# Five transposes of a pipelined graph network: from the tensor engine to 32x32 block turns on the vector engine and copies by DMA

## The reference

```
x = layernorm(x + L0(x, adj))   # attention, 8 heads of 16, edge bias, then W_o
x = layernorm(x + L1(x, adj))   # convolution of 17 taps, exp(-distance) messages, GRU gates
x = layernorm(x + L2(x, adj))   # additive attention: u = adj*exp(e_i+f_j), normalised by rows
x = layernorm(x + L3(x, adj))   # graph attention, 4 heads of 32, leaky relu, masked softmax
```

## Time and profile before

| | |
|---|---|
| median of three runs | 1429.56 us (1428.88 to 1431.28) |
| profiled execution, its own time | 1432.08 us |
| its span | 1430.3 us |
| mean granted TensorE clock | 0.976 |
| busy: PE, DVE, ACT, POOL | 1352.1, 1191.3, 1188.4, 663.1 us |
| DMA | 46.86 MB, 33 GB/s |

### The profile page before, as it was taken

The page is one execution under the profiler, slowest core; times in us unless marked ns, Lnnn a source line. Parts: engine busy times, 40 slices in busy tenths (PEclk is TensorE's granted clock), DMA queues, the critical chain, the costliest instruction groups (busy, mean ns, idle before and its releaser), DMA issues.

```text
span 1430.3 us, 40514 instructions
## 1 busy us (share of the span) xinstructions
PE 1352.1 (95%) x13178; PEld 1075.1 (75%) x13267; DVE 1191.3 (83%) x3407; ACT 1188.4 (83%) x4353; POOL 663.1 (46%) x1014
## 2 busy tenths in 40 slices
PE   4799999999999999999999999999999999999964
PEld 3577788877778887777888777788877778887642
DVE  6568888888888888888888888888888888886763
ACT  3867888889888888998888899888889988887654
POOL 1133445554444555444455544445554444555532
PEclk7899999999999999999999999999999999999986
DMA  3100110011111001111100111111011111100000
GB/s 117 38 31 31 31 31 17 16 39 38 39 38 39 25 16 39 38 38 39 39 29 12 39 39 38 38 39 34 6 39 39 38 39 38 33 8 16 9 15 23
DMA packets 23825, 46.86 MB, mean 33 GB/s; under 512 B 2753, under 2 KB 2754, under 8 KB 23490
## 3 DMA queue, kind: packets, MB, share of 16 engines
q1 hardware_dynamic: 23618, 44.27, 9.8%
HBM read 35.88 MB, written 8.39 MB: 31 GB/s over the span
## 4 chain that ended last, share of the span: by engine, by line
PE 78%; DVE 10%; POOL 5%; issue 4%; ACT 3%; DVEq 0%; POOLq 0%; ACTq 0%
PE B L591 18%; PE B L689 14%; PE B L499 12%; PE B L537 5%; PE B L558 4%; DVE B L1353 4%; DVE x L1326 3%; POOL rstd L376 3%; PE B L808 2%; PE B L523 2%; PE B L788 2%; PE B L754 2%; PE B L581 2%; PE B L665 2%; PE B L683 2%
## 5 line engine op out<-in xcount | busy, mean ns | idle before, releaser
L995 ACT ACTIVATE e<-B,nm 128x128 f32<-128x128 f32 x1024 | 363.9, 385 | 12.5 <-DVE nm L1361 12.0
L499 PEld LDWEIGHTS B<-ident,e 128*128 128x128 f32 x1536 | 187.0, 144 | 104.3 <-issue 75.7
L499 PE MATMUL B<-ident,e 128*128 128x128 f32 x1536 | 230.0, 281 | 9.2 <-ACT e L1151 3.9
L995 ACT ACTIVATION_READ_ACCUMULATOR e<-B,nm 128x1 f32 x1024 | 231.9, 226 | 0.0
L1353 DVE SCALAR_TENSOR_TENSOR B<-an,rowb,mask 128x512 f32<-128x512 f32 x256 | 194.2, 794 | 19.0 <-ACT pT L1004 9.5
L1151 ACT ACTIVATE e<-l,nm 128x128 f32<-128x128 f32 x512 | 198.9, 400 | 10.0 <-DVE nm L1582 9.9
L1361 DVE TENSOR_REDUCE nm<-B 128x4 f32<-128x512 f32 x256 | 166.5, 683 | 35.0 <-PE B L537 34.8
L1004 ACT ACTIVATE pT<-B 128x512 f32<-128x512 f32 x256 | 157.9, 617 | 44.5 <-PE B L499 41.3
L373 POOL TENSOR_TENSOR veps<-meanv,eps 128x4 f32<-128x4 f32 x128 | 41.8, 326 | 328.9 <-DVE meanv L1320 328.8
L376 POOL TENSOR_TENSOR rstd<-veps,neghalf 128x4 f32<-128x4 f32 x128 | 139.7, 1092 | 10.0
L1582 DVE TENSOR_REDUCE nm<-l 128x4 f32<-128x512 f32 x128 | 87.0, 679 | 41.9 <-ACT l L1141 41.9
(11 more groups left out here) (201 smaller groups left out, 3471.1 us busy)
## 6 DMA issues: line engine op xcount, KB each, us to landing
xt<-in_x_t SPq DMA_DIRECT2D x32, 256.0 KB, 3.1
an<-in_adj_n SPq DMA_DIRECT2D x32, 256.0 KB, 2.7
xn<-in_x_n SPq DMA_DIRECT2D x32, 256.0 KB, 3.3
at<-in_adj_t SPq DMA_DIRECT2D x32, 256.0 KB, 3.2
out_x<-xo SPq DMA_DIRECT2D x32, 256.0 KB, 3.5
wm<-in_mats SPq DMA_DIRECT2D x1, 1088.0 KB, 9.4
wm<-in_mats SPq DMA_DIRECT2D x1, 832.0 KB, 7.1
wm<-in_mats SPq DMA_DIRECT2D x1, 320.0 KB, 3.0
```

What stands on the lines that cost most here:

```text
L499: last = mm(g(dst, b), g(src, b), ident[:, :], is_transpose=True, start=(b == 0), stop=True, skip_group_check=True)
L995: last = fn(g(e0[:, h % 2, :], b), g(bank, b), ACT.Exp, bias=nm0[:, h % 4, b:b + 1], accum_out=sum0[s % 2][:, b, head(h):head(h) + 1])
```

## The change

The turn is split in two. DVE turns each 32x32 block of a tile in itself (`v.transpose`, in the order rows STREAM_TRANSPOSE), which leaves the blocks in their old places. DMA then moves the blocks: the tile is written whole to DRAM (128 rows of 2 KB, `write_blocks`) and read back in four transfers (`read_blocks`), one for each 32 partitions, in which every run of 32 numbers, 128 bytes, goes to its new place: 4 x 32 x 4 x 4 = 2048 runs a tile. For the inverse sums it is one turn of a 128x32 tile, four small writes and one read that repeats each row for 16 partitions. The tiles `x1b`, `yb`, `x3b`, `o3b`, `recb` take the turned blocks, `yn` and `o3n` the moved ones. `turn_out3` reads the PSUM bank directly, so the copy `keep_out3` goes as well.

Gone are five tile transposes a group on PE, four copies a group on ACT and `spread_sums` on POOL. DVE gets five turns a group. SP gets 25 DMAs a group, with waits between write and read. The order of every engine's step is written anew, with other bank assignments.

```diff
+            def write_blocks(s, done, sent, got, here, there):
...
+                wait(sp, q[got], MOVED * s)
+                sp.wait_ge(q[done], s + 1)
+                sp.dma_start(there[:, :], here[:, :]).then_inc(q[sent], DMA)
+
+            def read_blocks(s, sent, got, there, here):
+
+                sp.wait_ge(q[sent], DMA * (s + 1))
+                for c in range(4):
+                    sp.dma_start(here[32 * c:32 * c + 32, :].rearrange("r (b i j) -> r b i j", b=GB, i=4),
+                                 there.rearrange("(i r) (b c j) -> c r b i j", i=4, b=GB, c=4)[c]).then_inc(q[got], DMA)
+
+            def write_sums(s):
...
+                for i in range(4):
+                    sp.dma_start(inv_mem.rearrange("h (b i j) -> i (h b) j", b=GB, i=4)[i],
+                                 recb[32 * i:32 * i + 32, :]).then_inc(q["rb_sent"], DMA)
+
+            def read_sums(s):
...
+                sp.dma_start(recT[:, :], inv_mem.unsqueeze(1).broadcast_to([H0, D0, GB * N])).then_inc(q["recT_got"], DMA)
...
+            def read_x1(s):
...
+                wait(sp, q["v1_done"], s)
+                wait(sp, q["zx_done"], s)
...
+                wait(sp, q["ghn_ps"], s)
+                read_blocks(s, "x1_sent", "x1T_ready", x1_mem, x1T)
...
             def step(t):
+                write_x3(t - 5)
+                read_x3(t - 5)
+                load_at(t - 3)
+                write_y(t - 4)
+                read_y(t - 4)
+                write_out3(t - 6)
+                store(t - 8)
                 load_xt(t)
+                load_xn(t - 1)
                 load_an(t)
-                load_xn(t)
-                store(t - 8)
-                load_at(t - 1)
+                read_out3(t - 6)
+                write_x1(t - 2)
+                read_x1(t - 2)
+                write_sums(t - 1)
+                read_sums(t - 1)
...
-                pe.wait_ge(ln_out[0], s + 1)
-                transpose4(bank, x1).then_inc(q["x1t_ps"], 1)
...
-                pe.wait_ge(q["x1T_ready"], s + 1)
+                pe.wait_ge(q["x1T_ready"], MOVED * (s + 1))
                 mm(bank[:, :], wm[:, W1:W1 + N], x1T[:, :], start=True, stop=True).then_inc(q["c1_ps"], 1)
...
-                fn(x1T[:, :], bank[:, :], ACT.Copy).then_inc(q["x1T_ready"], 1)
...
+            def turn_x1(s):
...
+                wait(dve, q["x1_sent"], DMA * s)
+                dve.wait_ge(ln_out[0], s + 1)
+                v.transpose(x1b[:, :], x1[:, :]).then_inc(q["x1b_done"], 1)
...
+            def turn_out3(s, bank):
...
+                wait(dve, q["o3_sent"], DMA * s)
+                dve.wait_ge(q["pv3_ps"], s + 1)
+                v.transpose(o3b[:, :], bank[:, :]).then_inc(q["o3b_done"], 1)
```

More of the change, by code:

```diff
@@ L43 @@
 DMA = 16
-STEPS = GROUPS + 16
+MOVED = 4 * DMA
+STEPS = GROUPS + 8
 (C_G1, C_B1, C_M1, C_V1, C_G2, C_B2, C_M2, C_V2, C_BIR, C_BIZ, C_BIN, C_BHR, C_BHZ, C_BHN, C_A1, C_A2,
@@ L561, in values @@
                 last.then_inc(q["pv_ps"], 1)
-            def sums_T(s, bank, users):
-                if not live(s):
-                    return
-                freed(pe, s, users)
-                pe.wait_ge(q["recx_done"], s + 1)
-                for b in range(GB):
-                    last = mm(g(bank, b), recx[:, b, :, :].rearrange("p h d -> p (h d)"), ident[:, :], is_transpose=True,
-                              start=(b == 0), stop=True, skip_group_check=True)
-                last.then_inc(q["recT_ps"], 1)
             def project_out(s, bank, users):
@@ L1111, in exp_edges @@
                 fn(eg[:, :, :], h2[:, :, N:HC], ACT.Exp).then_inc(q["eg_ready"], 1)
-            def keep_x3(s, bank):
-                if not live(s):
-                    return
-                wait(act, q["h3_ps"], s)
-                wait(act, q["ej_ps"], s)
-                act.wait_ge(q["x3t_ps"], s + 1)
-                fn(x3T[:, :], bank[:, :], ACT.Copy).then_inc(q["x3T_ready"], 1)
             def keep_h3(s, bank):
@@ L1488, in gru_out, with turn_y, stats1 @@
                 v.tensor_tensor(yT[:, :], zn[:, :], zx[:, :], ALU.add).then_inc(q["y_done"], 1)
-            def stats1(s, bank):
+            def turn_y(s):
+                if not live(s):
+                    return
+                wait(dve, q["y_sent"], DMA * s)
+                dve.wait_ge(q["y_done"], s + 1)
+                v.transpose(yb[:, :], yT[:, :]).then_inc(q["yb_done"], 1)
+            def stats1(s):
                 if not live(s):
@@ L1500, in aggr1, with norm1 @@
                 ln_aggregate(1, s)
[L1502 removed]
+            def norm1(s):
                 if not live(s):
@@ L1572, in norm2, with turn_x3 @@
                     return
-                wait(dve, q["x3t_ps"], s - 1)
+                wait(dve, q["x3b_done"], s - 1)
                 wait(dve, q["r3_done"], s - 1)
                 ln_apply(2, s, r2, x3[s % 2])
+            def turn_x3(s):
+                if not live(s):
+                    return
+                wait(dve, q["x3_sent"], DMA * s)
+                dve.wait_ge(ln_out[2], s + 1)
+                v.transpose(x3b[:, :], x3[s % 2][:, :]).then_inc(q["x3b_done"], 1)
             def row_max3(s, b):
@@ new lines, in step @@
+                stats3(t - 8)
+                row_max(t - 2, 7, B[7])
+                stats1(t - 5)
+                aggr3(t - 8)
+                invert_sums3(t - 7)
+                aggr1(t - 5)
+                row_max3(t - 6, 0)
+                row_max3(t - 6, 1)
+                hidden_bias(t - 5, (B[6], B[0]))
+                edge_mask3(t - 3)
+                norm1(t - 5)
+                norm0(t - 3)
+                turn_x1(t - 3)
+                hidden_times_e(t - 5)
+                norm3(t - 8)
```

663 lines of the change are left out of this document (321 added, 342 removed).

## The result

The kernel after takes 1462.45 us (median of four runs, 1461.5 to 1463.6) against 1429.62 us before on the same chip: ratio 1.0227, 95% interval [1.0214, 1.0241]. It is 2.3% slower; the forecast was 1413, 1.2% faster.

The account below looks back on a forecast made before the run. PE was taken to bound the kernel before, DVE after: 39.33 us plus 0.9 stall gives a 40.2 us period. 32 x 40.2 plus ends of 126.8 is a 1413.2 us span, forecast 1413 us, range 1380 to 1485.

Parts of the forecast that it names:

- What bounds the kernel: Middle of the kernel before: PE's own work, 41.15 of a 41.64 us period; other engines have 4.6 us or more spare.
- PE's new need, 38.95 us a period: PE in each period: 41.15 us less 2.2 for five tile transposes taken away.
- DVE's work, 39.33 us: DVE in each period: 36.78 us plus 2.55 for the five turns, making DVE the new floor.
- The stall, 0.9 us between 0 and 2.4: Each period: waits between nearly full DVE and PE, added to the 39.33 us floor for a period of 40.2.
- the sum: Whole kernel: 32 periods of 40.2 us plus ends of 126.8 us give a span of 1413.2 us.
- the likeliest case: Whole kernel: the forecast itself, chance 0.45, 1394 to 1429 us with stalls between 0.3 and 1.4 us.
- Reading `o3n` and `yn` from SBUF: DVE operations that read these tiles from SBUF instead of a bank: costed at nothing.
- The round trip and its cover: Tile through DRAM: 8.5 us with turn, write 3.5 and read 4.3; covered by other work in the middle.
- The rival of slow reads: Reads in 128-byte runs take 7.8 us and PE waits at `embed`: period 42.15, 1489 us, chance 0.29.
- The ends: Pipeline's fill and end: 97.8 us before plus four uncovered trips of 7.3 us, 126.8 us.
- The rival "coupling": Middle: DVE and PE wait on each other 1.4 us a period; period 40.7, span 1429, no change; chance 0.13.
- The range, 1380 to 1485: Whole kernel's time in us, set to leave out 2 in 10; upper end just short of the slow-reads case's end.

Follow-up runs that it names:

- h2: Kernel before with only the inverse sums moved from PE transposes to a DVE turn and DMA: 1429.8 us, ratio 0.9998 to before.
- e3: Kernel after with both the norm of x1 ahead of `row_max3` and the fifth edge seed behind `residual0`: 1427.6 us, ratio 0.9986 to before.
- e1: Kernel after with one DVE call moved, the norm of x1 (`norm0`) ahead of `row_max3`: 1447.4 us, ratio 1.0129 to before.
- e2: Kernel after with one DVE call moved, the fifth edge seed behind `residual0`: 1442.6 us, ratio 1.0098 to before.
- h1: Kernel before with only layer 3's outputs moved to a DVE turn and DMA, `divide3` reading SBUF: 1479.9 us, ratio 1.0345 to before.
- e6: Kernel after with each block read made one plain transfer of 128 rows of 2 KB (tiles wrongly arranged): 1448.5 us, ratio 1.0134 to before.
- h3: Kernel before with both the inverse sums and layer 3's outputs moved to DVE turns and DMA: 1455.7 us, ratio 1.0183 to before.
- e7: e3 with POOL's `zx` made to wait until the first four edge seeds are written: 1459.9 us, ratio 1.0221 to before.
- e10: e3 with `aggr0`, `aggr2` and `turn_x3` each moved one place later in DVE's step: 1435.4 us, ratio 1.0038 to before.

## Why the prediction was wrong, point by point

- **What bounds the kernel: the step that failed.** "So the middle is PE's own work" and "2.3 us is all that the period could fall". h2 refutes it for one tile: 0.435 us off PE and 0.21 onto a DVE with 4.6 to spare gave 0.02. DVE's path from `divide3` through the norm of x3 was within 0.07 us of PE's, and the idle time of a whole period said nothing of that stretch.
- **PE's new need, 38.95 us a period.** Read as 40.1 after and 39.9 in e3. The difference is in the records missing before and in short waits that count as busy, so the step can't be judged by the busy time.
- **DVE's work, 39.33 us: measured 39.44.** The turn was sized rightly: 0.71 us long, the next operation 0.64 after its start. Neither half nor double. But two errors cancelled in the sum. Seeds beside POOL cost 0.13 us more each (8 x 0.13 = 1.0 us a period), which the forecast did not have. Other work ran shorter than before, the norms above all (a mean of 341 ns for 425 over the eight operations of x1 and x3, 0.66 us a period).
- **The stall, 0.9 us between 0 and 2.4: measured 2.28.** This is the mis-sized term: 1.4 us a period, or 44 of the 46.6 us by which the span missed the sum (1459.8 for 1413.2). The sum took it from PE's 0.49 us of idle time before. In DVE's row it is 1.09 for the hole ahead of `row_max3`, about 1.0 in the short gaps, and 0.18 for PE. e1 took the hole away with no turn removed, so it belongs to the order of DVE's step. The gaps cost nothing as long as DVE had 4.8 us to spare, and the forecast had no term for them once its row was full. 2.28 lies within the bounds 0 to 2.4 of this term, but not within the 0.3 to 1.4 that the likeliest case was given.
- **The collision with POOL was in no rival.** e2 shows it with one call moved (20 us). The Trainium skill (SBUF — State Buffer, Who interferes with whom) states it: a DVE instruction with two SBUF inputs, or in some fast modes, contends with a GpSimd instruction that reads SBUF, and whoever issues first gets the shared ports for its whole instruction. By that rule `divide3` was safe as long as it read a PSUM bank and is exposed since it reads `o3n`, which is what e1 and h1 show (0.69 us beside `zx` from a bank, 1.70 from SBUF); the forecast weighed a rule on DMA and not this one.
- **Reading `o3n` and `yn` from SBUF "at nothing".** True in the kernel after (679 ns for 692 of a bank), and the trap in e1, e3 and h1, where the same operation takes 1.05 to 1.71 us beside `zx`.
- **The round trip and its cover: right.** Writes 2.0 to 2.6 us (I took 3.5), the four reads of a tile 0.65 apart (those of x3 up to 0.94) and 2.4 to landing, 4.4 us in all (I took 4.3), and no wait for a DMA in the middle. The rival of slow reads is refuted by e6, and the rule of the Trainium skill (DMA: Bandwidth & Descriptors, Specifications) on 512 bytes changed nothing in the middle here: a quarter of a tile in runs of 128 bytes landed in 2.4 us, four at once, and with 281537 packets under 512 bytes all packets together took 33% of the 16 engines' time.
- **The ends: 126.8 forecast, 124.8 measured.** The last trip runs from the turn at 1443.96 to its use at 1451.63, 7.7 us (the sum took 8.5). That the whole agrees is partly luck: the sum has four trips, and e6 speaks for about seven that are exposed in part:

```profile
1443.96 0.72 DVE L1623 STREAM_TRANSPOSE o3b<-B 128x512 f32<-128x512 f32 x1 [6.78 <-PE B L875]
...
1451.63 0.69 DVE L1631 TENSOR_TENSOR r<-o3n,rec 128x512 f32<-128x512 f32 x1 [3.07 <-DMA o3n<-o_mem]
```

- **The rival "coupling"** (period 40.7, 1429 us) named the right mechanism with 0.13 and too small a size: "before, 0.49 us was all PE lost" was taken as evidence against it, and it was the weakest reading of all. With e3's order the kernel is at 40.52 and 1427.6, near this rival's 1429; but what is left there is DVE's full row and not waits from engine to engine, so the agreement is a coincidence.
- **The range, 1380 to 1485, holds 1462 by luck.** Its upper end stands there for the rival of slow reads, which e6 refutes. The forecast itself, faster with 0.58, failed in direction.

Open: how much of its 0.435 us PE would have kept without the turn on DVE in h2, what the short gaps are worth by themselves, why h3 loses less than h1, and whether a place for `divide3` exists that makes h1 or h3 faster than before. e3 is the fastest kernel of all, by 0.14% [0.03, 0.25]: hardly more than a tie.

## What to carry to other kernels

An engine at 99% is a bound only if shortening it shortens the loop: take one cheap piece off it (h2) before moving five, and look whether the piece lands anew in the stretch that the engine waits for. Idle time summed over a period says nothing of such a stretch: with 4.6 us idle, DVE had 0.07 us to spare there. A nearly full engine also pays for the short gaps between dependent operations, here 1 us a period. When work is moved onto such an engine, ask for each of its long SBUF operations what POOL does beside it; reading a PSUM bank, or waiting for another engine, may be what keeps them apart. Transfers that share one queue in program order wait for each other's releases, so a later operand on one trip (e7) delays another.

## What the runs showed of the hardware that was not expected

- A vector operation with two inputs in SBUF and a POOL tensor operation hold each other up. The one that starts clearly later pays: the seed that started 0.60 us behind `xd` took 1.61 us for 0.75. When the two start within 0.02 us of each other either can pay: `yT<-zn,zx`, which started at 737.50 together with `xd`, kept its 0.68 while `xd` took 1.66 (1.34 in the kernel before), and in e3 the one at 882.22 took 1.65 beside an `xd` of 1.12 from 882.20. `r<-o3n,rec` went from 0.68 to 1.70 and `r<-r,x` from 0.68 to 1.80 beside `zx`, `tr<-tr`, with one input, from 0.41 to 0.98, and the norm of x1 in e10 from 1.12 to 1.51 beside `aT`. Row maxima, operations on a PSUM bank and the 32x32 turns kept their length (0.65 to 0.71 us). The rule of the Trainium skill named above agrees with all of these (`tr` and the norms would fall under its fast modes, which no run here tests); the prices are this case's.
- A turn of 128x512 float32 takes 0.71 us from SBUF or from a bank, about as long as other passes over 512 columns here (0.68 to 0.75).
- Between a DVE operation and the one whose result it reads stands a gap of about 0.1 us (729.92 to 730.03 in after), in all about 1 us a period.
- An issue of a block read takes SP 0.65 us (2.60 / 4), against 0.33 for the plain write of a tile, from the timeline of SP's queue after. The four of x3 took 3.75 us together at 736.82. That the pattern's number of dimensions is the cause is not shown: the small writes of the inverse sums, 32x32 each, also take 0.69 (2.76 / 4).

```profile
708.34 0.33 SPq L317 DMA_DIRECT2D o_mem<-o3b  x1
...
716.14 2.60 SPq L323 DMA_DIRECT2D o3n<-o_mem  x4
```
